# Decoder kernel on one core: where context keys and values are made, where the causal mask is applied, and in which order the maxima's rows are loaded

## What is computed

```
x = x + mamba(layernorm(x))
x = x + attention(layernorm(x), context)     # context: 1024 tokens of width 128
x = x + ffn(layernorm(x))

# attention, 16 heads of 16
y  = softmax(causal(q k^T / 4)) v            # q, k, v   from x with biases bq, bk, bv
y += softmax(qc kc^T / 4) vc                 # qc from x; kc, vc from the context, biases bck, bcv
return y @ Wp + bp
```

## Time and profile before

| | us |
|---|---|
| three runs | 2013.3, 2014.9, 2007.1 |
| median | 2013.3 |
| the profiled execution | 2016.16 |
| its span, first to last instruction | 2014.4 |
| PE busy | 1555.1 (77%) |
| DVE busy | 1374.3 (68%) |
| ACT busy | 834.3 (41%) |
| POOL busy | 654.8 (33%) |

### The profile page before, as it was taken

How to read it: one execution, slowest core, us unless ns; L and a number is a source line. 1 busy time by engine, 2 the same in 40 slices (tenths; PEclk the granted TensorE clock), 3 DMA queues, 4 the chain that set the end, 5 groups by cost and what they waited for, 6 DMA issues and landing times. The chain is left out here.

```text
span 2014.4 us, 19539 instructions
## 1 busy us (share of the span) xinstructions
PE 1555.1 (77%) x6696; PEld 750.1 (37%) x6696; DVE 1374.3 (68%) x2056; ACT 834.3 (41%) x1570; POOL 654.8 (33%) x423
## 2 busy tenths in 40 slices
PE   5796789884986789874977798855557898669985
PEld 2353322231553322242544222222233222348874
DVE  5997577648995767468986777389966765333334
ACT  4541346655441255645432366643313456322211
POOL 2664401222863401125653211227644021112221
PEclk9898789996997899987998799978988899779998
DMA  5910621003000630002003510021006210227754
GB/s 162 345 55 0 154 64 41 1 0 116 17 0 23 162 73 3 1 31 99 3 0 88 130 40 1 1 84 44 0 0 157 48 33 1 64 98 245 232 179 127
DMA packets 123491, 147.44 MB, mean 73 GB/s; under 512 B 18117, under 2 KB 106190, under 8 KB 121344
## 3 DMA queue, kind: packets, MB, share of 16 engines
q1 hardware_dynamic: 119648, 137.53, 24.4%
q0 software_dynamic: 3744, 8.66, 1.2%
HBM read 96.79 MB, written 50.79 MB: 73 GB/s over the span
## 5 line engine op out<-in xcount | busy, mean ns | idle before, releaser
L168 PE MATMUL PS<-arena 128*32 128x512 f32 (+10 forms) x4150 | 885.4, 457 | 124.4 <-ACT arena L1734 31.6
L168 PEld LDWEIGHTS PS<-arena 128*32 128x32 f32 (+3 forms) x4150 | 372.8, 128 | 615.0 <-ACT arena L1734 274.3
L1734 ACT ACTIVATE arena<-PS 128x512 f32<-128x512 f32 (+3 forms) x768 | 375.7, 541 | 321.1 <-PE PS L168 319.4
L1347 POOL TENSOR_TENSOR arena<-arena 128x1024 f32<-128x1024 f32 x128 | 305.1, 2384 | 235.8 <-DVE arena L1373 140.8
L1777 DVE TENSOR_REDUCE maxs<-PS 128x1 f32<-128x1024 f32 x256 | 303.9, 1219 | 82.8 <-PE PS L168 82.3
L1373 DVE TENSOR_TENSOR_SCAN arena<-PS,arena 128x1024 f32<-128x1024 f32 x128 | 292.2, 2283 | 6.1 <-ACT PS L1322 6.1
L168 PE MATMUL PS<-arena,ident 128*128 128x512 f32 (+1 forms) x560 | 261.7, 594 | 5.4 <-DVE arena L1382 5.4
L1322 ACT ACTIVATE PS<-arena,A_neg 128x511 f32<-128x511 f32 x256 | 165.9, 681 | 232.0 <-DVE arena L1373 183.9
L1503 POOL TENSOR_TENSOR arena<-xn 128x512 f32<-128x512 f32 x16 | 20.2, 1265 | 530.4 <-ACT xn L1723 530.4
L1382 DVE TENSOR_TENSOR arena<-arena,PS 128x1024 f32<-128x1024 f32 x128 | 156.3, 1221 | 7.7 <-PE PS L168 3.7
L1781 DVE TENSOR_REDUCE maxs<-PS 128x1 f32<-128x512 f32 (+3 forms) x256 | 108.5, 484 | 61.5 <-PE PS L168 60.8
(11 more groups left out here) (260 smaller groups left out, 1751.2 us busy)
## 6 DMA issues: line engine op xcount, KB each, us to landing
arena<-in_ew SPq DMA_DIRECT2D x46, 512.0 KB, 4.8
arena<-stack_parts SPq DMA_DIRECT2D x288, 64.0 KB, 2.4
rows_in<-nil SPq DMA_DIRECT2D x16, 1088.0 KB, 12.5
arena<-b_rows SPq DMA_DIRECT2D x16, 1024.0 KB, 7.6
stack_parts<-arena SPq DMA_DIRECT2D x40, 384.0 KB, 3.1
arena<-stack_parts SPq DMA_DIRECT2D x96, 128.0 KB, 4.5
arena<-rows_in SPq DMA_DIRECT2D x23, 272.0 KB, 5.1
arena<-picked_rows SPq DMA_DIRECT2D x16, 256.0 KB, 3.7
```

Of the source, the lines that this page charges most:

```text
L168: return nc.tensor.matmul(o, l, r, start=start, stop=stop)
L1347: nc.gpsimd.tensor_tensor(b_sb[i % 2], u[:, 2 * kh:2 * kh + 2, :], Brow[:, n, :].unsqueeze(1).to_broadcast([P, 2, T]), ALU.mult).then_inc( ...
L1734: nc.scalar.activation(probs[(HG * s + h) % NPR][:, 0:N], bank(4 + n % 2)[:, 0:N], ACT.Exp, scale=HD ** -0.5).then_inc(S["ring_read"], 1)
```

## The change

- The context keys of the first half of the heads are multiplied at the end of `scan`, into banks 0 and 1 (banks of the decay factors, free after the last but one unit). `TILES` begins with these two tiles, and their parts, stores and loads come first everywhere.
- The eight value tiles of the context stand right behind the `out_w` products, ahead of the turning of `xn`. Value tiles are now read by ACT, without bias.
- The biases: `v_bias` (loaded by eight small DMAs in the first `scan`) times `wp` is summed by 8 products in the first `attend`, DVE adds the sum to `bp`, and PE waits for that ahead of the turning (sequence 0 only).
- POOL clears only the part of `V` and `VC` behind the column of ones, and `ones_rows(0)` waits for the four tiles of `xn` where it waited for the `out_w` products.
- The causal mask leaves PE: POOL sets the weights above the diagonal to zero in `probs` (`affine_select`, 128 x 128, one for each head of each causal step), and `values` waits for it. `x1 + bp`, `ones_rows(1)` and `ones_rows(2)` stand behind the masks of group 0.
- On SP the maxima's causal rows of group 0 are loaded ahead of the last store and of all four stacks of group 1; before, twelve loads of group 1 stood ahead of them.
- `max_rows_out(g + 1, CAUSAL)` stands ahead of the scores of heads 2 and 3 of its step; group 0 spreads its jobs 4, 2, 3, 3 where it had 3, 3, 3, 3.

```diff
@@ gpsimd
-                pool.wait_ge(S["v_init"], 3)
-                pool.wait_ge(S["outproj_mm"], TT)
-                ones_rows(0)
+                for i in range(CK_TILES):
+                    low(i)
+                pool.wait_ge(S["xn_ready"], TT)
+                pool.wait_ge(S["parts_ready"], CK_TILES)
+                pool.wait_ge(S["v_init"], 1)
+                ones_rows(0)
...
+                for k in range(TT):
+                    masks(0, k)
+                if b == 0:
+                    pool.wait_ge(S["bp_ready"], 1)
                 link(nc.gpsimd.tensor_tensor(x1[:], x1[:], bp[:].unsqueeze(1).to_broadcast([P, TT, DM]), ALU.add))
-                pool.wait_ge(S["parts_ready"], len(TILES))
+                pool.wait_ge(S["masked"], HG * TT)
                 ones_rows(1)
@@ masks, new
+                def masks(g, k):
+                    for h in range(HG):
+                        pool.wait_ge(S["ring_read"], ring(g, k, h) + 1)
+                        own = probs[(HG * (STEPS * g + k) + h) % NPR][:, 0:P]
+                        nc.gpsimd.affine_select(out=own, in_=own, compare_op=ALU.is_ge, fill=0.0, base=0,
+                                                pattern=[[1, P]], channel_multiplier=-1).then_inc(S["masked"], 1)
@@ steps of the tensor program
-                        n = (3 if k < TT + 4 else 2) if g == 0 else 2
+                        jobs = list(range(done, done + JOBS_AT[g][k]))
...
                         scores(g, k, (0, 1))
-                        if late_rows:
+                        if turn_context:
                             max_rows_out(g, CONTEXT)
+                        if turn_causal:
+                            max_rows_out(g + 1, CAUSAL)
```

More of the change, by code:

```diff
@@ L88, in decoder @@
         bqk = sb("bqk", [P, 4, KM])
[L89 to L90 removed]
+        v_bias = sb("v_bias", [P, 2, NG])
         wp = sb("wp", [P, NG, DM])
@@ L756, in experts_vector @@
             mixed(NB - 1)
-        TILES = [(x, hh, half) for hh in range(2) for x, half in ((0, 0), (1, 0), (2, 0), (3, 0), (3, 1))]
+        TILES = [(x, 0, half) for x, half in ((3, 0), (3, 1), (0, 0), (1, 0), (2, 0))]
+        TILES += [(x, 1, half) for x, half in ((0, 0), (1, 0), (2, 0), (3, 0), (3, 1))]
         CS = 2 * TT
@@ L1305, in tensor @@
                         power(i - POW_AT)
+                pe.wait_ge(S["h_done"], len(UNITS) - 1)
+                pe.wait_ge(ctx_loaded, 16 * (b + 1))
+                if b == 0:
+                    pe.wait_ge(load_later, 16 * (len(LATER) + NG * HG + 2 * HG))
+                for i in range(2):
+                    mm(bank(i), wck[:, 0:P], ctxT[:, i * T:(i + 1) * T], True, True)
             def scalar(act):
@@ L1390, in attend @@
             HEADS_IN = 16 * 2 * 6
-            FIRST_TILES = 6
+            CK_TILES, FIRST_TILES = 2, 6
+            TILE_BANKS = (0, 1, 6, 7, 4, 5, 6, 7, 6, 7)
+            VALUE_ORDER = list(range(TT, 3 * TT)) + list(range(TT))
             def tile_bank(i):
-                return bank(2 + i) if i < FIRST_TILES else bank(6 + i % 2)
+                return bank(TILE_BANKS[i])
             def job(i):
@@ L1501, in gpsimd @@
                 for g in range(NG):
+                    if g + 1 < NG:
+                        masks(g + 1, 0)
+                        masks(g + 1, 1)
                     pool.wait_ge(S["ring_read"], ring_den(g, 1) + 1)
@@ L1675, in tensor @@
                             values(g, k - 1)
-                        for i in rest:
-                            if i == KJOBS:
-                                max_rows_out(g + 1, CAUSAL)
+                        for i in jobs[len(early):]:
                             max_job(g + 1, i)
-                    done = 0
                 values(NG - 1, STEPS - 1)
@@ L1698, in middle, with value_tile @@
                     nc.scalar.activation(pt[i % NPT][:, 1, :], r_sb[i % 2], ACT.Copy).then_inc(S["mid_ready"], 1)
-                for i in range(len(TILES)):
-                    high(i)
-                    if 1 <= i < FIRST_TILES:
-                        middle(i - 1)
-                    if i >= FIRST_TILES - 1:
-                        middle(i)
+                def value_tile(j):
+                    t = VALUE_ORDER[j]
+                    act.wait_ge(S["v_mm"], j + 1)
+                    dst = V[:, t, :, 0:HD] if t < TT else VC[:, t - TT, :, 0:HD]
+                    nc.scalar.activation(dst, bank(2 + j % 2)[:, 0:DM].rearrange("p (h d) -> p h d", h=H), ACT.Copy)\
+                        .then_inc(S["v_ready"], 1)
+                high(0)
+                high(1)
+                middle(0)
+                middle(1)
+                act.wait_ge(S["v_init"], 1)
+                for j in range(2 * TT):
+                    value_tile(j)
+                act.wait_ge(S["xT_mm"], 2)
+                nc.scalar.activation(xT[:, 0, :], bank(0), ACT.Copy).then_inc(S["xT_ready"], 1)
+                for i in range(CK_TILES, CK_TILES + 3):
+                    high(i)
+                    middle(i)
+                for j in range(2 * TT, 3 * TT):
+                    value_tile(j)
+                for i in range(FIRST_TILES - 1, len(TILES)):
+                    high(i)
+                    middle(i)
                 def copy_context(g):
```

192 lines of the change are left out of this document (91 added, 101 removed).

## The result

| | before | changed kernel |
|---|---|---|
| median of the runs, us | 2014.1 | 1934.1 (1932.1 to 1937.3) |
| ratio, 95% interval | | 0.961, 0.9584 to 0.9637 |
| span of the profiled execution | 2014.4 | 1935.5 |
| PE busy | 1555.1 | 1519.7 |
| POOL busy | 654.8 | 716.3 |

A forecast was written before the change was run, and what follows sets the result against it. No engine was taken as full; a chain through all bounds the kernel. Terms 11.0 + 1.0 - 1.8 + 2.3 + 1.4 = 13.9 us per attend, 55.6 for four, less 4.5, give 51: 2013.3 to 1962, range 1940 to 1990.

The forecast's parts named there:

- The fill of ones: Head of attend: POOL's fill leaves the normalisation, L433 falls from 3.43 to 0.17, `xn` is ready 3.7 us earlier.
- DVE's unbroken run of context maxima: Group 0, causal to context turning: DVE no longer idles between its 16 maxima; 22.0 us forecast for four attends.
- The masks: Causal steps: mask matmuls leave PE; of 2.9 us at most per attend, half was taken, 1.4.
- The selects: Causal steps: POOL's selects last about 0.31 us each, are used one step later and stay hidden.
- The bias products: Sequence 0, ahead of the turning: eight products on PE's path cost 4.7 us at most; 4.5 taken once.
- one instruction was held: Behind group 0's context turning: cast L1797 waits for a POOL memset, costing 1.8 us per attend.
- part 4: Steps of groups 1 to 3: the earlier causal turning covers PE's 0.77 to 0.78 us idle for `mrest`; 2.3 us per attend.
- half clock at the first jobs: First maximum jobs: PE idles some 4 us ahead of them, so 2.0 us per attend was added.
- For `out_w`: Head: PE's idling falls from 4.33 to about 2.3 us; products save up to 2.9 us, 1.0 taken per attend.
- The position of the queries: Head: the queries start at 636.0 instead of 639.78, 3.8 us earlier.
- Rival (b): Whole kernel: no instruction held, `out_w` at full clock, all masks counted; 72 us less, 1941; chance 0.12.

The follow-up runs named there:

- before_ones: Kernel before with one edit: the fill of ones `ones_rows(0)` stands behind `xn`; measured 0.9934 of the kernel before, 13 us less.
- ones_early: Changed kernel with the fill of ones put back beside the normalisation, waiting for the `out_w` products; 0.9691 of the kernel before.
- best_clock: clock_up plus bias products in PE's pause for the stacks and later fills of ones for groups 1 and 2; 0.9477 of the kernel before, median 1912.5.
- before_turns: Kernel before with only the causal maxima's turn ahead of the scores of heads 2 and 3, and jobs 4, 2, 3, 3; 0.9884, 23 us less.
- clock_up: Changed kernel with products that nobody reads in two pauses of PE; 0.955 of the kernel before, median 1922.6.
- best_two: best_clock with group 2's fill of ones also held until group 1's maxima's parts are ready; 0.9499 of the kernel before, median 1914.6.
- before_rows: Kernel before with one edit: twelve loads of group 1 stand behind the maxima's rows on SP; 0.9932 of the kernel before, 14 us less.

## Why the prediction was wrong, step by step

**What was right.** The chain that it read (fill of ones, `xn`, queries, stacks, maxima, rows) is the one that moved. The fill of ones was taken at 3.7 per attend, 15 in all, and measures 3.4 per attend in before_ones, 13 in all; that ones_early gives 16 is luck (6.2 in three attends and 1.0 in one). DVE's unbroken run of context maxima was forecast to save 5.5 in its stretch and saved 6.0 to 8.4. The masks were taken at 1.4 per attend and measure 1.3 in their own stretches, 4 us in all where the total doesn't resolve them. The selects lasted 0.29; PE's loads of weights waited for them 27 times, 7.2 us in all four attends and 0.4 at most, where the prediction had said never. The bias products were taken at 4.5 and cost 4.0 (the first turning stood 5.7 behind that of best_clock, 1.7 of it `out_w`'s clock). Behind group 0's context turning one instruction was held, for 1.3 us where 1.8 were taken; the two casts that are held 0.9 us each in groups 1 and 2 were not foreseen.

That the cast waits for the memset (1.50 for 0.21) and the next one, L1830, whose two inputs lie in SBUF, takes 0.28 as elsewhere, was the point weighed against the Trainium skill (page "SBUF — State Buffer", section "Who interferes with whom"): by its rule only the first is held by a writing GpSimd instruction, and the trace agrees with both halves.

**First failed step: part 4, "which then cover the 0.77 to 0.78 us", 2.3 us per attend.** It is the largest error, 8 to 14 of the 28 us: the move measures 17 to 23 where 9 were taken. The term priced the pause at its own length and put what stands behind it at nothing. A turn costs 1.03 at full clock instead of 0.77, since ACT runs dry in the pause. In the kernel before the clock also falls behind one of the two pauses in groups 1 and 2, which costs 1.5 us of busy time in each attend, and in group 0, where it is 0 to 4.8. And a pause was left as it stood ("where 0.98 was waited anyway"), which in before_turns is 0.59. The prediction watched the clock in the head, behind pauses of 3.4 us and more, and not in the steps, where it falls behind the pause of 0.77 at 754.12 that stands in the earlier trace rows.

**Second: one attend was read and multiplied by four.** The stretch between group 0's two turnings took 27.3 in the second attend, but 29.3, 27.6 and 29.6 in the others. In the changed kernel all four take 21.1 to 21.6. This alone is 4.7 us, which a look at the other three would have shown before.

**Third: the clock of the head.** The forecast added 2.0 per attend for a half clock at the first jobs, behind a pause of 4 us; the pause came (3.75), and from the first job to the causal turning it was 2.6, 1.1, 1.3 and 1.1 more than the 11.06 of before, 1.5 on average. For `out_w` it took 1.0 of 2.9; it was 2.7 in the second attend and 0 in the third, 1.3 on average. The position of the queries was 0.4 better than forecast, 0.2 of it a slip (633.9 + 1.1 + 0.8 is 635.8 and not 636.0), and the time from them to the first job 0.6. Together that is the 7 us which the first two rows of the table have above the forecast.

**Fourth, not resolved: the terms were added as if they were independent.** Three of them are worth 50 to 54 us singly and 63 together, within the intervals of the runs. Rival (b), "all goes well", gave 1941 and was nearest, for a reason it didn't contain.

**Open.** Whether `out_w` runs at 7.14 or 8.83 in the changed kernel behind the same pause of 2.62 differs from attend to attend and from run to run, and no run here shows what decides it. The same holds for group 3 (31.1, 32.4 or 34.2, and 35.4 in one attend of clock_up and one of best_two).

## What to carry to other kernels

A wait of TensorE had two prices in this kernel: its own length, and the half clock of what stood behind it, which was as large (14.0 of 24.2 us in before_turns) but not in every attend. So cost both, count a short wait at full value or more even in the middle of dense work, and fill pauses that can't be removed with idle products: three 128x512 products and two more in each attend gave 12 us here. Read every repetition of a stage before multiplying one. The order of transfers mattered here only where the queue was busy at the moment that the urgent one became ready. And read a total that fits stretch by stretch: in ones_early and before_rows the right total hid stretches that were off in both directions.

## What was not expected of the hardware

- TensorE behind a pause of 2.62 us ran 32 instructions in 7.14 or in 8.83 (in other runs also in between); with the pause at 1.43, in 7.14 or 7.15 each time (four attends each of clock_up, best_clock and best_two).
- Products whose result nobody reads shortened the program by 12 us (0.961 to 0.955), and a 16x128 cast on VectorE waits out 1.3 us of a GpSimd memset that touches only three partitions.
- The same 445 matmuls took 76.11 us of busy time at a mean clock of 0.98 and 74.61 at 1.00: of two pauses of 0.77 in a stretch of 85 us, one was followed by 3.4 us at half clock.
